# Attention's product of exponentials and values, in column strips of TensorE instead of one added 72-row block

## What is computed

```python
x = x + jnp.tanh(g_xattn[0]) * _L0_xattn_ref(_layernorm(x, axis=-1), ctx_512, ctx_512)
# in both: scores of grouped queries against the keys, softmax, product with the values
scores = jnp.einsum('bkgsd,bktd->bkgst', qh, kh) * scale
attn = jax.nn.softmax(scores, axis=-1)
out = jnp.einsum('bkgst,bktd->bkgsd', attn, vh)
```

## Time and profile before

| | us |
|---|---|
| median of 3 runs | 1719.53 |
| lowest, highest | 1709.69, 1721.87 |
| span of the profiled execution | 1714.7 |
| attention of layer 0 in it | about 20 to 298 |
| attention of layer 1 in it | about 1168 to 1520 |

### The profile page before, as it was taken

One profiled execution on the slowest core, in us unless ns is written; L12 is line 12 of the kernel. 1 busy time (PEld: TensorE's weight loads), 2 busy tenths in 40 slices (PEclk: granted clock), 3 DMA queues, 4 the chain that ended last, 5 costly groups with the idle time before them and its releaser, 6 DMA issues.

```text
span 1714.7 us, 32329 instructions
## 1 busy us (share of the span) xinstructions
PE 1178.8 (69%) x9122; PEld 778.6 (45%) x9132; DVE 1084.7 (63%) x2699; ACT 783.1 (46%) x1599; POOL 883.5 (52%) x846
## 2 busy tenths in 40 slices
PE   4999998133333299999678777871676777846775
PEld 2566665112221266666555555650454444532243
DVE  5899996666666466666444454442765555747898
ACT  3566665122222166666445454441343333433574
POOL 2343343266666633333377777715888888516100
PEclk9999999555555599999777887785788888878878
DMA  9555554032323599999899999984344434100011
GB/s 209 161 151 154 148 154 135 15 115 104 111 106 110 154 281 308 310 301 304 206 242 237 252 246 248 247 199 101 53 54 55 55 55 55 28 1 1 13 37 49
DMA packets 283470, 247.09 MB, mean 144 GB/s; under 512 B 117584, under 2 KB 270032, under 8 KB 282960
## 3 DMA queue, kind: packets, MB, share of 16 engines
q1 hardware_dynamic: 234192, 169.99, 38.9%
q0 software_dynamic: 49152, 75.53, 20.8%
HBM read 111.93 MB, written 117.77 MB: 134 GB/s over the span
## 4 chain that ended last, share of the span: by engine, by line
DMA 24%; DVE 20%; PE 18%; POOL 16%; issue 13%; SPq 4%; ACT 3%; DVEq 1%; POOLq 0%; ACTq 0%
DMA xs<-V 13%; POOL x L632 11%; DMA arena<-xs 8%; PE bank L1493 4%; DVE arena L1318 3%; DMA xs<-arena,V 2%; PE bank L1369 2%; POOL rs L575 2%; PE bank L1381 2%; DVE arena L971 2%; PE bank L1355 2%; PE bank L1569 2%; PE bank L1370 2%; SPq L518 2%; DVE arena L1316 2%
## 5 line engine op out<-in xcount | busy, mean ns | idle before, releaser
L632 POOL DMA_INDIRECT x<-ys,idx x256 | 404.1, 1578 | 129.2 <-issue 57.6
L650 POOL DMA_INDIRECT xs<-V x192 | 187.1, 974 | 207.7 <-DMA xs<-V 188.5
L1493 PE MATMUL bank<-arena,region 128*128 128x128 f16 x2496 | 253.2, 245 | 1.6 <-ACT arena L834 0.9
L834 ACT COPY arena<-bank 128x640 f16<-128x640 f16 x192 | 132.3, 689 | 190.2 <-PE bank L1569 188.2
L1569 PE MATMUL bank<-arena 128*128 128x128 f16 x1440 | 145.2, 240 | 105.3 <-DMA arena<-xs 101.5
L1381 PE MATMUL bank<-arena 128*72 128x256 f32 (+1 forms) x768 | 212.0, 417 | 0.1
L1493 PEld LDWEIGHTS bank<-arena,region 128*128 (+1 forms) x2496 | 187.0, 111 | 19.2 <-issue 6.2
L1569 PEld LDWEIGHTS bank<-arena 128*128 128x128 f16 x1440 | 97.0, 107 | 113.3 <-DMA arena<-xs 85.4
L573 POOL TENSOR_TENSOR ve<-mv,epsilon 128x1 f32<-128x1 f32 x96 | 39.5, 412 | 202.0 <-DVE mv L912 180.0
L1381 PEld LDWEIGHTS bank<-arena 128*72 128x72 f32 (+1 forms) x768 | 117.2, 158 | 46.4 <-issue 13.5
L982 DVE TENSOR_REDUCE arena<-bank 128x8 f32<-128x512 f32 x192 | 124.1, 675 | 15.5 <-PE bank L1355 14.3
(11 more groups left out here) (204 smaller groups left out, 2557.6 us busy)
## 6 DMA issues: line engine op xcount, KB each, us to landing
ys<-arena SPq DMA_DIRECT2D x96, 512.0 KB
arena<-xs SPq DMA_DIRECT2D x288, 160.0 KB
xs<-idx SPq DMA_DIRECT2D x52, 256.0 KB, 2.4
arena<-in_wpairs SPq DMA_DIRECT2D x32, 256.0 KB, 2.6
arena<-in_wpairs SPq DMA_DIRECT2D x128, 64.0 KB, 2.5
x<-ys,idx POOLq DMA_INDIRECT x256, 6.3
out<-arena SPq DMA_DIRECT2D x16, 256.0 KB, 2.2
xs<-idx SPq DMA_DIRECT2D x52, 64.0 KB, 2.1
```

What stands on the lines that cost most here:

```text
L632: pool.indirect_dma_start(tile_x(t), None, ys[t // HT], bass.IndirectOffsetOnAxis(ap=idx[:, t, k:k + 1], axis=0), compute_op=ALU.add).then ...
L650: pool.indirect_dma_start(xs[t // HT], bass.IndirectOffsetOnAxis(ap=at_row[:, t, n % 8:n % 8 + 1], axis=0), ROW[t % NROW], None).then_inc( ...
L834: act.copy(XTP[g % 2][q], tpm[n % 2]).then_inc(R_["xt"], 1)
L1493: mm = pe.matmul(o, lhs(a, w, k), rhs(a, w, k), start=(n == 0), stop=(n == 3 * KT - 1))
```

## The change

Each pair of heads gets its own strip of array columns and so its own PSUM rows: cg = 128 / npair, 32 columns in layer 0 and 64 in layer 1. Within a strip each head has 128 / nk columns (16 or 32): its value channels first, then its column of ones, then zeros. Nothing is added over pairs, so each matmul starts and stops its own result. Number, order and moving operands of the matmuls stay. PVS becomes 128 rows instead of w, and its four transposes, whose moving operand is the identity, take 128 columns instead of 72 or 68. ACT's and DVE's instructions keep their element counts per partition and change their strides; the two copies into PVS run on 128 partitions. VD shrinks from 288 to 128 columns per batch, and with it POOL's two memsets before each attention. No wait is added or removed.

```diff
-    VD = [carve([2, 4 * W0]) for _ in range(2)]
+    VD = [carve([2, P]) for _ in range(2)]
...
-                        pool.tensor_copy(VD[j][:, b, 0:npair * w].rearrange("p (n w) -> p n w", w=w)[:, :, C:w],
-                                         ones.rearrange("p (n k) -> p n k", k=nk)).then_inc(a["vd_set"], 1)
+                        pool.tensor_copy(VD[j][:, b, :].rearrange("p (k w) -> p k w", k=nk)[:, :, d], ones).then_inc(a["vd_set"], 1)
...
-                    at = v[half * S:(half + 1) * S, 0, half * d:(half + 1) * d]
-                    return bass.AP(at.tensor, at.offset, [list(at.ap[0]), [4 * W0, 2], [w + 2 * d, npair], [1, d]])
+                    return v[half * S:(half + 1) * S].rearrange("p b (n h w) -> p b n h w", h=2, w=P // nk)[:, :, :, half, 0:d]
...
-                        act.copy(PVS[0:w].rearrange("p g (b s) -> p g b s", b=2),
-                                 bank[6][0:w, :].rearrange("p (b g s) -> p g b s", b=2, g=G)).then_inc(a["pvs_ready"], 1)
+                        act.copy(PVS.rearrange("p g (b s) -> p g b s", b=2),
+                                 bank[6][:, :].rearrange("p (b g s) -> p g b s", b=2, g=G)).then_inc(a["pvs_ready"], 1)
...
-                        o = bank[7][:, 0:G * w].rearrange("p (g w) -> p g w", g=G)
+                        o = bank[7].rearrange("p (g k w) -> p g k w", g=G, k=nk)
                         dve.wait_ge(a["ot_ready"], t)
-                        dve.reciprocal(RC[:, :, 0:nk], o[:, :, C:w]).then_inc(a["rc_done"], 1)
+                        dve.reciprocal(RC[:, :, 0:nk], o[:, :, :, d]).then_inc(a["rc_done"], 1)
...
-                        dve.tensor_tensor(heads(ON[1 - j]), o[:, :, 0:C].rearrange("p g (k d) -> p g k d", d=d),
+                        dve.tensor_tensor(heads(ON[1 - j]), o[:, :, :, 0:d],
                                           RC[:, :, 0:nk].unsqueeze(3).to_broadcast([P, G, nk, d]), ALU.mult).then_inc(a["on_ready"], 1)
...
+                    cg = P // npair
                     for p in range(npair):
                         e = EX[(b * nsc + p // 2 + (0 if nsc == 2 else 2 * j)) % 4]
-                        mm = pe.matmul(bank[6][0:w, b * 256:(b + 1) * 256], VD[j][:, b, p * w:(p + 1) * w],
-                                       e[:, (p % 2) * 256:(p % 2 + 1) * 256], start=(p == 0), stop=(p == npair - 1))
+                        mm = pe.matmul(bank[6][p * cg:(p + 1) * cg, b * 256:(b + 1) * 256], VD[j][:, b, p * cg:(p + 1) * cg],
+                                       e[:, (p % 2) * 256:(p % 2 + 1) * 256], start=True, stop=True)
...
-                            mm = pe.transpose(bank[7][:, g * w:(g + 1) * w],
-                                              PVS[0:w, g, :], ident[0:w, 0:w])
+                            mm = pe.transpose(bank[7][:, g * P:(g + 1) * P], PVS[:, g, :], ident)
```

More of the change, by code:

```diff
@@ L60, in const_columns @@
     at, out = 0, {}
-    for name, width in (("ident", P), ("ones0", 4 * 8), ("ones1", 2 * 4)):
+    for name, width in (("ident", P), ("ones0", 8), ("ones1", 4)):
         out[name] = (at, width)
@@ L77, in attention_table @@
     for layer, (nk, d) in enumerate(LAYERS):
-        pair = np.arange(nk // 2)[None, :, None]
-        head = 2 * pair + (r[:, :, None] >= S)
-        put(f"ones{layer}", np.arange(nk)[None, None, :] == head)
+        put(f"ones{layer}", np.arange(nk)[None, :] % 2 == (r >= S))
     return t
```

## The result

The change made the kernel slower. The median went from 1716.62 us (4 runs, 1709.69 to 1721.87) to 1734.56 us (4 runs, 1729.94 to 1744.73); the ratio of after to before is 1.0148, with a 95% interval of 1.0113 to 1.0184. The profiled execution of after spans 1742.9 us, against 1714.7 before.

The account below looks back on a forecast made before the run. TensorE and VectorE were taken to tie in layer 0's middle, POOL to bound layer 1. -3.4 + 3.6 - 1.3 + 1.0 = -0.1 us took the median from 1719.53 to 1719.4 us; range 1709 to 1737.

Parts of the forecast that it names:

- strips that don't overlap: Rival for the values' f32 matmuls: eight rounds stay and changes come on top, +18 us, 1737 us; chance 0.12.
- the middle of layer 0: Tiles 4 to 27: values off the chain, longer PVS transposes cost +0.15 us each, +3.6 us in all.
- full overlap: Rival for the values' matmuls: all four strips stream at once, two rounds, total -4.4 us, 1715 us; chance 0.12.
- the clock falls: Rival in layer 0's middle: about 1 us idle per tile lowers TensorE's clock, +22 us, 1741 us; chance 0.10.
- the clock rival: Layer 0's middle: TensorE drops to its 1.2 GHz level once per tile, +22 us, 1741 us; chance 0.10.
- Rounds: Values' calls: five rounds instead of eight in layer 0, saving 0.65 us; three instead of four in layer 1, 0.22 us.
- Changes between strips and full width: TensorE in layer 0: three new changes per tile at about 0.12 us, taken as 0.35 us.
- The price of a low clock: Layer 0's middle: 1.4 us lost per tile, about a third hidden in idle space, 0.9 x 24 = +22 us.
- The transposes: PVS transposes in layer 0's middle: 0.19 us longer per tile, +0.15 us on the chain, 24 tiles.
- Start of layer 0: Tiles 0 to 3: values on the chain, gains capped by VectorE's idle time, -3.4 us in all.
- End of layer 0: Tiles 28 to 31: shorter products in the last two tiles, less longer transposes, -1.3 us in all.
- Layer 1: 0 while POOL's gathers set the pace; about four tiles after them +0.2 to +0.4 us each, +1.0 in all.

Follow-up runs that it names:

- fill2: The changed kernel with each layer-0 call's strip products issued twice into the same place; ratio to before 1.0011 (0.994 to 1.0082).
- turn128: The kernel before, product unchanged, with the four PVS transposes made 128 by 128 and PVS zeroed once per attention; ratio to before 1.005 (0.9951 to 1.0149).
- fill3: The changed kernel with each layer-0 call's strip products issued three times into the same place; ratio to before 1.0027 (0.9975 to 1.0079).
- strips_l0: The changed kernel with strips in layer 0 alone, layer 1 as before; ratio to before 1.0276 (1.0085 to 1.0467).

## Why the prediction was wrong

The forecast was 1719.4 us, no change; measured was 1.5% more. The median, 1734.56 us, lies in the range, 1709 to 1737, by luck: the upper bound came from strips that don't overlap, and they overlap fully. What happened is a case that had a chance of 0.12 joined to one of 0.10.

**The step that failed** is the middle of layer 0, which the sum has at +3.6 us, with five rounds per call and the clock held. Measured: two rounds, a clock of 0.87 where it was 1.00, and +28.0 us (205.36 to 233.40). The mistake behind it is that the rivals "full overlap" and "the clock falls" were priced apart. Full overlap was given 1715 us with the clock held, the clock rival 1741 with an idle space of 1 us. But the first makes the second: with two rounds the pair ends 2.1 us earlier (forecast 0.9, full overlap 2.2), the idle space becomes 2.25 us, and at that 19 of 25 tiles were slow. With an idle space of 1.5 us, in fill2, "no change" is what was measured.

**Rounds.** Forecast five, from the order A0 B0 A1 B1 that I supposed; measured two. The program holds one matmul per pair, and the two passes of f32 appear only in the trace; there the eight starts come as four within 0.02 us and four more 0.24 us later. The order of the passes within a strip was no limit. The Trainium skill has this in TensorE: Matmul & The Clock Gate, Measured speedup vs the span model: matmuls in different strips take the time of one plus about 4 ns each. The trace agrees: the eight in 0.64 us are one MATMUL of 0.40 and one more round of 0.24, and within a round the starts lie 7 ns apart. It counted among my rivals with 0.12 and deserved the most.

**Changes between strips and full width.** Forecast three per tile, 0.35 us in all. L1418 to L1378 is 0.58 us where it was 0.50, L1431 to L1378 0.56 where it was 0.44: 0.08 and 0.12. The change back to full width costs more: L1378 to L1431 is 0.66 us, of which two rounds take 0.43, so 0.22. About 0.4 in all, nearly right.

**The price of a low clock.** Forecast 1.4 us lost, 0.9 after hiding, in every tile: 22 us. Measured 1.6 us in 18 tiles more, 28 us. The low stretch is not hidden in the idle space: all 15 between 66 and 265 us begin 0.5 to 1.5 us after the idle space has ended, and fall on the maxima and scores that the chain runs through.

**The transposes.** Forecast +0.15 in 24 tiles, 3.6 us; measured 0 (turn128). I read the 0.15 in place of 0.11 at 103.53 as the only wait on exponentials and overlooked that the score product right behind the transposes waits too.

**Start of layer 0.** Forecast -3.4 us, from VectorE's idle time ahead of L904 in three tiles (1.03, 2.41, 0.72) and ahead of L982 in a fourth. The three waits are gone in after, but L904 (L900 there) takes longer without them, 1.96 to 2.04 us in place of 1.08 to 1.24:

```profile
35.95 1.31 POOL L606 TENSOR_TENSOR region<-arena,region 64x512 f16<-64x512 f32 x1 [0.18 <-POOL region L603]
36.17 2.04 DVE L900 TENSOR_TENSOR KL<-region,KH 64x896 f16<-64x896 f32 x1
45.80 1.96 DVE L900 TENSOR_TENSOR KL<-region,KH 64x896 f16<-64x896 f32 x1
55.25 2.04 DVE L900 TENSOR_TENSOR KL<-region,KH 64x896 f16<-64x896 f32 x1
```

Wait and instruction together took 2.11, 3.49 and 1.96 us in before, so 0.1, 1.5 and nothing were won; the periods of these tiles moved by as much (9.89 to 9.76, 11.05 to 9.53, 9.51 in both). The idle time ahead of an instruction was the wrong cap, as its own time did not stay. The trace shows with what it goes: without the wait L900 starts while POOL's L606 runs, and it ends 0.95 us after L606 has ended (37.26 to 38.21; 0.94 and 0.95 in the other two). In before the wait let most of POOL's instruction (L609 there) pass:

```profile
58.34 1.31 POOL L609 TENSOR_TENSOR region<-arena,region 64x512 f16<-64x512 f32 x1 [0.18 <-POOL region L606]
```

This one ends at 59.65 and L904, 1.24 us long from 59.35, 0.94 us later; the two L904 of 1.08 us overlap none. So VectorE had a wait for POOL behind the one for ScalarE. No run moved POOL's work to test that. The fourth tile, the sixth period, went from 9.88 to 9.72 us, as the clock fell there in after; in fill3 it takes 8.16. All of the first four periods together gave -2.0 us between the profiles, and -1.2 to -2.2 against the kernels without strips in layer 0.

The first q_ready came 1.3 us earlier, which I had priced at 0. POOL's memsets and copies for VD are followed by an idle time and then by its first work. POOL in before and in after:

```profile
8.33 0.66 POOL L591 COPY arena<-cst 128x32 f32<-128x32 f32 x4
16.79 0.18 POOL L573 TENSOR_TENSOR ve<-mv,epsilon 128x1 f32<-128x1 f32 x1 [7.81 <-issue]
```

```profile
7.08 0.56 POOL L585 MEMSET arena<- 128x256 f32 x2 [2.19 <-DMA gate<-in_g_ffn]
7.71 0.58 POOL L589 COPY arena<-cst 128x8 f32<-128x8 f32 x4
15.48 0.18 POOL L571 TENSOR_TENSOR ve<-mv,epsilon 128x1 f32<-128x1 f32 x1 [7.19 <-issue]
```

All kernels with the small VD have the first q_ready at 19.5 to 20.0 us, those with the large one, strips_l0 too, at 21.1 to 21.4. So it goes with the size of VD. But the copies end only 0.7 us earlier in after than in before, and the idle time behind them is shorter too, 7.19 in place of 7.81 us (6.9 to 7.8 over all kernels). The trace has two MODIFY_POOL_CONFIG instructions at its start and then nothing of POOL; no run tells what sets its length.

**End of layer 0.** Forecast -1.3. From the last q_ready to the end of the last PVS transposes it is 13.53 us where it was 14.57, so -1.0. About right.

**Layer 1.** Forecast 0 under POOL and +1.0 in the tail. Measured 331.48 against 331.02 us, and 331.12 for strips_l1; from the last q_ready to the last output projection 14.01 against 13.85. Right, within what the runs tell.

**What bounds the middle.** Right: TensorE and VectorE tied at 8.15 us, and a shorter product won nothing there.

## What to carry to other kernels

When TensorE is tied with another engine, work taken off it becomes idle space, and ask what the granted clock does then before asking what is won; price a rival with what it does to the other rivals. Idle space may be harmless where real work divides it: one wait that moved 1.8 us of work into the middle was worth 1.7% here. Once the path has room on TensorE, look for the other engine's own wait, since only that turned the room into time here. A wait that goes away is a gain only if the instruction behind it keeps its time, so look at what the other engines do then.

## What the runs showed of the hardware

- Four f32 matmuls of 128 rows by 32 columns, 256 moving columns, in four strips take 0.64 us together; four of 72 columns, added one after another, took 1.89 us. In layer 1 two of 64 columns take 0.65 us at the higher clock, two of 68 took 1.03.
- A change from full width to strips costs 0.08 to 0.12 us, a change back about 0.2.
- The granted clock fell at 2.25 and 1.97 us of idle space per 8 us tile in one piece, held at 1.5 us, fell with 0.98 and 1.22 us around 0.6 us of work, and held with 1.1 and 1.17 us around 1.8 us of work. The kernel with two pieces around 1.8 us and the one with 2.25 us in one have the same busy time, 5.9 us in an undisturbed tile of 8.15.
- A slow tile lost 1.6 us, and the fall came 0.5 to 1.5 us after the end of the idle space.
- A VectorE subtraction of 64 x 896 elements took 1.08 us alone and 1.24 to 2.04 us where it started while a POOL instruction of 64 x 512 ran; it then ended 0.94 to 0.95 us after POOL's end, four times of four.
